# The additive key mask of a block-diagonal attention: its row moved from the key blocks into the dense operand

## The reference

```python
q = (layernorm(x) @ Wq + bq)   # 16 heads of 8, per batch
k = (ctx @ Wk + bk)
v = (ctx @ Wv + bv)
score = einsum('bhqd,bhkd->bhqk', q, k) / sqrt(8)
score = where(key_padding_mask, -1e30, score)
x = x + (softmax(score) @ v) @ Wo + bo
x = x + experts(layernorm(x))   # top 2 of 8, 512 hidden units, exact gelu
```

## Time and profile before

| what | us |
|---|---|
| median of 3 runs | 787.57 |
| lowest and highest run | 782.49, 789.75 |
| the profiled execution | 786.22 |
| its span, first to last instruction | 784.5 |
| PE busy | 626.8 (80%) |
| DVE, ACT, POOL busy | 560.7, 543.2, 494.1 |

### The profile page before, as it was taken

How to read it: one execution, slowest core, us unless ns; L and a number is a source line. 1 busy time by engine, 2 the same in 40 slices (tenths; PEclk the granted TensorE clock), 3 DMA queues, 4 the chain that set the end, 5 groups by cost and what they waited for, 6 DMA issues and landing times.

```text
span 784.5 us, 18253 instructions
## 1 busy us (share of the span) xinstructions
PE 626.8 (80%) x4964; PEld 480.8 (61%) x4964; DVE 560.7 (71%) x1813; ACT 543.2 (69%) x1060; POOL 494.1 (63%) x892
## 2 busy tenths in 40 slices
PE   1788888888888988889898527799999999999400
PEld 0465656666666666657566425688888888888300
DVE  4577788777788888887887545477777777777346
ACT  3477778777777878777777426588888888888200
POOL 8343467767576767675767763377777777677700
PEclk9999999999999999999999858899999999999855
DMA  4766777668577877676764246887787777774088
GB/s 140 221 193 188 228 218 222 184 210 241 162 208 226 242 227 200 207 218 193 182 209 126 82 127 216 264 253 244 242 253 244 249 239 253 236 244 139 1 294 348
DMA packets 118905, 164.24 MB, mean 209 GB/s; under 512 B 22479, under 2 KB 77286, under 8 KB 118823
## 3 DMA queue, kind: packets, MB, share of 16 engines
q1 hardware_dynamic: 88711, 126.14, 51.9%
q10 hardware_dynamic: 21024, 20.06, 9.5%
q0 software_dynamic: 9088, 17.07, 6.7%
HBM read 73.07 MB, written 33.92 MB: 136 GB/s over the span
## 4 chain that ended last, share of the span: by engine, by line
PE 48%; DMA 21%; issue 10%; ACT 7%; POOL 7%; SPq 4%; DVE 3%; ACTq 1%; POOLq 0%; DVEq 0%
DMA kb<-dense 12%; PE bank L1281 6%; PE bank L1254 5%; PE bank L1434 4%; PE bank L1432 4%; PE bank L1417 4%; PE bank L1420 4%; PE bank L1418 4%; PE bank L1433 4%; PE bank L1266 4%; DMA qb<-negm 3%; DMA qb<-yd 3%; POOL xd L538 2%; PE bank L1394 2%; PE bank L1242 2%
## 5 line engine op out<-in xcount | busy, mean ns | idle before, releaser
L638 POOL DMA_INDIRECT yd<-vs,idt x156 | 165.1, 1058 | 87.4 <-DVE vs L950 48.9
L695 DVE TENSOR_REDUCE mx<-bank 128x4 f32<-128x480 f32 x256 | 160.0, 650 | 47.9 <-PE bank L1254 47.4
L538 POOL DMA_INDIRECT xd<-rows,posi x128 | 128.9, 1007 | 88.4 <-DVE posi L801 58.6
L998 ACT ACTIVATE pt<-bank,mcol 120x512 f32<-120x512 f32 x256 | 171.6, 691 | 13.5 <-PE bank L1266 6.7
L936 DVE TENSOR_TENSOR qb<-hid,qb 128x512 fp32r<-128x512 f32 x156 | 109.7, 703 | 73.5 <-ACT hid L1148 72.4
L1145 ACT ACTIVATE qb<-bank,btile 128x512 fp32r<-128x512 f32 x156 | 107.6, 690 | 37.5 <-PE bank L1434 29.8
L1254 PE MATMUL bank<-kb,dense 128*128 128x480 f32 x256 | 87.5, 424 | 40.9 <-DMA kb<-dense 35.1
L1266 PE MATMUL bank<-qb,dense 128*120 128x512 f32 x256 | 100.5, 459 | 13.9 <-DMA qb<-negm 7.8
L1148 ACT ACTIVATE hid<-bank,btile 128x512 f32<-128x512 f32 x156 | 106.3, 681 | 0.0
L1030 ACT ACTIVATE ots<-bank 128x512 f32<-128x512 f32 x64 | 38.2, 597 | 69.5 <-PE bank L1281 69.5
L1254 PEld LDWEIGHTS bank<-kb,dense 128*128 128x128 f32 x256 | 46.1, 199 | 62.2 <-DMA kb<-dense 48.2
(11 more groups left out here) (169 smaller groups left out, 1515.4 us busy)
## 6 DMA issues: line engine op xcount, KB each, us to landing
kb<-wd SPq DMA_DIRECT2D x40, 512.0 KB, 5.2
qb<-wd SPq DMA_DIRECT2D x38, 512.0 KB, 5.0
qb<-dense SPq DMA_DIRECT2D x128, 128.0 KB
dense<-comp SPq DMA_DIRECT2D x64, 248.0 KB, 2.4
kb<-dense ACTq DMA_DIRECT2D x128, 120.0 KB, 3.5
rows<-xd SPq DMA_DIRECT2D x39, 264.0 KB, 2.8
wd<-wsp SPq DMA_DIRECT2D x16, 512.0 KB, 3.8
qb<-yd SPq DMA_DIRECT2D x16, 512.0 KB, 6.1
```

What stands on the lines that cost most here:

```text
L538: g.indirect_dma_start(xd, bass.IndirectOffsetOnAxis(ap=posi[r % 4][:, bk:bk + 1], axis=0), rows[r % 4][:, bk // 2, bk % 2, :], None, boun ...
L638: g.indirect_dma_start(yd, bass.IndirectOffsetOnAxis(ap=idt[k][:, j:j + 1], axis=0), yrow[p.parity][:, j, :], None, bounds_check=2 * NTOK ...
L695: v.tensor_reduce(mx[c % 2][:, :, gg, b], wide[m % 2][:, 0:J * KL].rearrange("p (j k) -> p j k", j=J), op=ALU.max, axis=AX.X).then_inc(w_f ...
L998: a.activation(pt[i % NP][:].rearrange("p j q -> p (j q)"), scores[t % 2][0:KL, :], ACT.Exp, bias=mcol[:, 2 * c + t // G:2 * c + t // G + ...
```

## The change

The mask row moves to pad row 31 of each block (rows 31, 63, 95 and 127 of `dense`), in the columns of the keys. SP writes it from `maskd` into `dense` in slot c-3, before `spread_high(c)`, and each of the four key blocks carries its own row along. In the dense queries the pad value 1 stands in these four rows (`mask_q`, the sum of four columns of the identity). So that the mask is not also multiplied with a 1 in the products by key, the query blocks copy 31 rows of each block instead of 32, and row 31 of `qb` keeps the zero it was cleared to. ACT's first key block waits for the mask row, which now has four semaphores. `kfirst` is gone, and PE waits for four key blocks.

```diff
-    NHI, NLO, MSK = 3, 7, 11
+    NHI, NLO, MSK = 3, 7, 31
...
+        mask_q = sb("mask_q", [P, 1])
...
-        mask_row = two("mask_row")
+        mask_row = four("mask_row")
...
             def mask_rows(c):
 
+                if c < ND:
+                    sp.wait_ge(dense_set, 2 * (c + 1))
+                else:
+                    sp.wait_ge(b_full, 8 * (c - ND + 1))
                 if c == 0:
                     sp.wait_ge(mask_dram, 16)
-                sp.wait_ge(kfirst[c % 2], 16 * (c // 2 + 1))
-                sp.dma_start(kb[c % 2][MSK:MSK + 1].rearrange("a j g n -> a (j g) n").bitcast(F32),
-                             maskd.bitcast(F32)[2 * c:2 * c + 2, :].rearrange("(a g b) k -> a g (b k)", a=1, g=1).to_broadcast([1, G * J, K2])).then_inc(mask_row[c % 2], 16)
+                sp.dma_start(dense[c % ND][MSK::R, :, N2:NK].bitcast(F32),
+                             maskd.bitcast(F32)[2 * c:2 * c + 2, :].rearrange("(a g b) k -> a g (b k)", a=1, g=1).to_broadcast([J, G, K2])).then_inc(mask_row[c % ND], 16)
...
                 for j in range(J):
-                    sp.dma_start(qb[c % 2][R * j:R * j + R, j, :, :].bitcast(F32),
-                                 dense[c % ND][R * j:R * j + R, :, 0:N2].bitcast(F32)).then_inc(qblk[c % 2], 16)
+                    sp.dma_start(qb[c % 2][R * j:R * j + R - 1, j, :, :].bitcast(F32),
+                                 dense[c % ND][R * j:R * j + R - 1, :, 0:N2].bitcast(F32)).then_inc(qblk[c % 2], 16)
...
-                if chunk(n + 2):
-                    mask_rows(n + 2)
...
                 if chunk(n + 3):
+                    mask_rows(n + 3)
                     spread_high(n + 3)
...
-                g.tensor_copy(dense[k][:, :, 0:N2], ident[:, MSK:MSK + 1].rearrange("p (g a) -> p g a", g=1).to_broadcast([P, G, N2])).then_inc(dense_set, 1)
+                g.tensor_copy(dense[k][:, :, 0:N2], mask_q[:, :].rearrange("p (g a) -> p g a", g=1).to_broadcast([P, G, N2])).then_inc(dense_set, 1)
...
-            pool.wait_ge(pad_set, 1)
+            pool.wait_ge(pad_set, 2)
...
+            v.tensor_reduce(mask_q[:, :], ident[:, MSK::R], op=ALU.add, axis=AX.X).then_inc(pad_set, 1)
...
+                    act.wait_ge(mask_row[c % ND], 16 * (c // ND + 1))
                 act.dma_start(kb[c % 2][R * j:R * j + R, j, :, :].bitcast(F32),
-                             dense[c % ND][R * j:R * j + R, :, N2:NK].bitcast(F32)).then_inc((kblk if j else kfirst)[c % 2], 16)
+                             dense[c % ND][R * j:R * j + R, :, N2:NK].bitcast(F32)).then_inc(kblk[c % 2], 16)
...
-                    pe.wait_ge(kblk[c % 2], 48 * (c // 2 + 1))
-                    pe.wait_ge(mask_row[c % 2], 16 * (c // 2 + 1))
+                    pe.wait_ge(kblk[c % 2], 64 * (c // 2 + 1))
```

More of the change, by code:

```diff
@@ L211, in moe_attention @@
         w_full, w_free = sem("w_full"), sem("w_free")
-        dn_in, qblk, kblk, kfirst, mrow = two("dn_in"), two("qblk"), two("kblk"), two("kfirst"), two("mrow")
+        dn_in, qblk, kblk, mrow = two("dn_in"), two("qblk"), two("kblk"), two("mrow")
         v_full, v_taken = sem("v_full"), sem("v_taken")
```

## The result

The changed kernel takes 1347.76 us (median of four runs, 1346.39 to 1348.28) against 785.03 before (four runs). The ratio is 1.717, with a 95% interval of 1.704 to 1.731: 562.7 us slower; 1355 us was forecast. Medians here are of all runs of a kernel; ratios and their intervals leave out runs more than 1.5% above its fastest. The profiled execution of after has a span of 1345.9 us, TensorE works in 55% of it, and the chain reads differently from the earlier trace rows.

What follows compares the result with a forecast made beforehand. Before: attention stage busy everywhere, full nowhere; key-block copy longest in the chain (12%). After: query blocks on one engine, 30.4 us per chunk; 56.4 + 942.4 + 6.2 + 347.7 + 1.7 = 1354.4, said as 1355 us, range 1200 to 1520.

Steps and rivals of the forecast that it cites:

- How 31 rows are dealt: Query-block transfers: the largest engine count up to 16 dividing the rows is used, so 31 rows run on one engine.
- The four on one engine, one after another: A chunk's four query blocks share one engine, 5.95 us each, 23.8 us per chunk; chance 0.83, around 1355 us.
- The rival of four engines: Query blocks run on four different engines beside each other: 10.5 us against SyncE's 8.0, 864 us at most; chance 0.04.
- The terms of the period: Attention stage, per chunk: packets 23.8, latency 1.7, other queues 2.2, SyncE issue 2.7; sum 30.4 us against 12.66.
- The price of a packet: Query-block packets of 1,024 bytes on one engine: taken as 48 ns each, from 44.3 to 48.8 in the trace.
- ScalarE's queue is not held up: Key-block issue stays as before; the rival, work coming after the transfer, gives 40.4 us a chunk, 1665 us, chance 0.05.
- the faster engine: Rival on query-block transfers: one engine moves 25.8 GB/s, nothing shared, period 24.1 us, total 1154 us; chance 0.03.
- the upper bound: Query blocks at 16.8 GB/s take 30.2 us; with the stage's other traffic on this engine, period 41.7, total 1711 us.
- What would show it: 1,920 fewer closing packets, maxima some 30 us apart, SyncE's long wait at maxima, DMA share below 0.4, mask-row wait gone.
- The mask's side alone: Moving the mask row out of the key blocks' path, without slow query blocks: -4 us, 783 us in all.
- the first rival: Query blocks of 31 rows dealt in rounded-up shares land as now; only the mask's side counts, 783 us; chance 0.05.
- A busy engine's cost to others: Sharing of the query blocks' engine: the sum adds 2.2 us per chunk for other queues, key blocks 1.5 of it.

## Why the prediction was right, and where it was not

- *How 31 rows are dealt.* Right. The one packet missing in the earlier trace rows fitted both dealings, as the prediction says, so no row decided between them before the run. The runs do: 31 rows close with one packet, 4 with 4, 15 with 15, 16 and 32 with 16. Rounded-up shares would have given 16 for 31. The rule of the Trainium skill that the prediction named (DMA: Bandwidth & Descriptors, "Why a DMA increments its semaphore by 16 and not by 1") agrees with every one of these counts.
- *The four on one engine, one after another.* Right: a share of 6.8% in the middle of a block, 23 to 25 packets a microsecond whichever queue they are of, and 28.2 us from the first block's issue to the maxima. The rival of four engines falls with it.
- *The terms of the period.* 30.4 us forecast, 30.32 measured. Transfer, other queues and latency were 23.8 + 2.2 + 1.7 = 27.7 against 28.2 in the slot shown; the issues afterwards 2.7 against 2.6 there. The first maxima row, forecast for 52.8, went out at 53.4. That it is so close is in part luck. The price of a packet was too high: on the busy engine q1 and q10 move 122 packets in 5 us, 41 ns each and not 48. At 41 ns the four blocks take 20.3 us, so that latency and all else on this engine took 7.9 of the 28.2 us and not the 3.9 of the sum; the two errors cancel. The 7 us by which 1355 is too high lie almost wholly behind the last product by key, where 341.5 us pass and not 347.7.
- *ScalarE's queue is not held up.* Right: its key blocks take 0.59 us to issue at the median, as in the kernel before, the next slot's work lies beside the transfer, and the period has no room for it twice. The 1154 us of the faster engine and the 1711 of the upper bound are far off too. (The prediction's 1160 us for the faster rate counts the gain on 31 chunks instead of 32; its own terms give 1153.)

```profile
L1077 ACTq DMA_DIRECT2D kb<-dense x128: 592/593/1620, 18.8 to 945.2; - x128
```

- *What would show it.* The closing packets, the 30 us between maxima, the share of 0.28 and the vanished wait at the mask row came as named. One sign was off: SyncE's wait at the maxima for `qb<-dense` is only 146.1 us, because it stands in the issue of the blocks most of the time (23% of the chain).

```profile
SPq L329 <- DMA qb<-dense: 146.1, 32, 11.1
```

- *The mask's side alone: wrong.* "I take -4: 783 us" was the price of the whole change under the first rival; the run with 32 rows measures 820. The step that failed is the sum of gain and loss there: the loss through loads beside the key blocks was named with 21 us and then more than cancelled, by a gain of at most 7.8 at the maxima rows and a choice inside the bounds. The wait for key blocks alone grew by 25.5 us, and the mask row's own place gave a few us at most (0.995, 0.991 to 0.999, with the wait put back). Had the blocks kept 32 rows, the range of that rival would have been missed.
- *A busy engine's cost to others* was counted on one side only. The sum has 1.5 us by which key blocks delay the query blocks; that the query blocks delay the key blocks is not in it, and under a period of 30 us it did not matter. With one block of 31 rows it made most of the 157 us: 133 are left when the loads are held back.

## What to carry to other kernels

Count the rows of a transfer before trimming one: here the number that is dealt over the engines counted for more than the bytes, and the partition that could be left out was cheaper copied. Look then at what the copied row does: here it lets the mask into the products by key a second time, which is harmless in these inputs because the mask is zero. A wait on an in-order queue can be of use to what it delays: here it kept bulk loads off a small transfer on the path, so before it is removed, look at which transfers it releases and what they will run beside. The place of bulk transfers in the slot was worth more than the wait that was to be saved: 3.5% lost by moving the loads, 1.8% gained by moving the store, and no more than a few us by the mask row's place.

## What the runs showed of the hardware that was not expected

- SyncE is held in the issue itself beside a busy engine. The four blocks of the slot shown take 15.32 us to issue instead of 2.65 in the run with 32 rows, and the load after them 5.63. When the fourth was issued (527.17), 12.9 us were left to the maxima, by estimate some 250 packets at the 19.8 per us of q1: SyncE runs about two such blocks ahead. That a queue of that engine was full is a reading of these times; no view shows its length. The prediction's sum did not need it, since the landing ends the loop anyway.
- Small transfers in flight beside a busy engine land when their share on that engine has: the mask row after 11.2 us beside blocks of 31 rows and after 2.5 beside blocks of 32. The Trainium skill (DMA: Bandwidth & Descriptors, "Queues, rings and completion order") says that an engine serves its queues in turn, packet by packet; the 13 packets of q10 beside 12 of q1 from 522 to 523 us agree with that.
- The Trainium skill advises to issue a DMA early and wait late (DMA: Bandwidth & Descriptors, "Rules for kernel authors"). Here an issue some 3 us earlier cost 35 us, since it met a transfer that was on the path, and one behind the spreads of the high parts cost 29.
